# Eight written-out layers on one core: turned sums of chosen tokens, key stores on ScalarE's queue, value sums behind the queries, loops written out

## The reference

```python
probs = jax.nn.softmax(logits, axis=-2)
vals_t, idx_t = jax.lax.top_k(probs.transpose(0, 2, 1), K)
tok = jnp.take_along_axis(x, flat_idx[:, :, None], axis=1)
merged = jnp.einsum('bked,bke->bed', tok, vals)
h = jnp.einsum('bei,eih->beh', jnp.concatenate([merged, ones], -1), w1)
h = jax.nn.gelu(h, approximate=False)
o = jnp.einsum('bej,ejo->beo', jnp.concatenate([h, ones], -1), w2)
```

## Time and profile before

| | |
|---|---|
| median of 3 runs | 3224.42 us (3224.24 to 3225.77) |
| profiled execution | 3221.38 us |
| its span, first to last instruction | 3219.5 us |
| mean granted TensorE clock | 0.937 |
| busy | PE 2746.0 us (85%), DVE 1872.5 (58%), ACT 1718.8 (53%), POOL 849.9 (26%) |
| mean DMA rate | 101 GB/s over the span |

### The profile page before, as it was taken

The page is one execution under the profiler, slowest core; times in us unless marked ns, Lnnn a source line. Parts: engine busy times, 40 slices in busy tenths (PEclk is TensorE's granted clock), DMA queues, the critical chain, the costliest instruction groups (busy, mean ns, idle before and its releaser), DMA issues. The chain is left out here.

```text
span 3219.5 us, 45933 instructions
## 1 busy us (share of the span) xinstructions
PE 2746.0 (85%) x14756; PEld 1541.0 (48%) x14850; DVE 1872.5 (58%) x4755; ACT 1718.8 (53%) x2876; POOL 849.9 (26%) x957
## 2 busy tenths in 40 slices
PE   7899869969999999676799878999757888888887
PEld 4233349824444454322322246999533444444453
DVE  6777551165555654323688640111459999999953
ACT  3566421146555555111277631333149999999953
POOL 4100020020000000011200031000338888888840
PEclk8899989989999999788799998999977999999988
DMA  5111156510000000696222162999250000000011
GB/s 172 47 53 48 48 184 217 194 56 1 1 1 1 1 1 1 259 416 277 72 56 66 54 232 84 341 343 347 82 155 11 21 27 18 20 20 21 17 30 49
DMA packets 161797, 325.35 MB, mean 101 GB/s; under 512 B 29392, under 2 KB 128464, under 8 KB 138448
## 3 DMA queue, kind: packets, MB, share of 16 engines
q1 hardware_dynamic: 152112, 303.14, 27.1%
q0 software_dynamic: 4608, 12.59, 1.2%
q10 hardware_dynamic: 4896, 7.35, 0.7%
HBM read 273.71 MB, written 49.15 MB: 100 GB/s over the span
## 5 line engine op out<-in xcount | busy, mean ns | idle before, releaser
L3178 DVE TENSOR_TENSOR_SCAN L3x_behind<-L3x_first_exp,L3x_beside_scan 128x513 f32<-128x513 f32 x256 | 309.3, 1208 | 0.0
L3058 POOL TENSOR_TENSOR L3x_fade<-L3x_behind,L3x_apart 128x1024 f32<-128x1024 f32 x128 | 280.8, 2194 | 68.8 <-DVE L3x_behind L3178 44.9
L1334 ACT ACTIVATE L1x_probs<-L1x_scores,L1x_neg_max 128x512 f32<-128x512 f32 x256 | 173.5, 683 | 218.7 <-DVE L1x_neg_max L1386 218.7
L1386 DVE TENSOR_REDUCE L1x_neg_max<-L1x_scores 128x2 f32<-128x1024 f32 x128 | 156.5, 1224 | 143.9 <-PE L1x_scores L1234 143.9
L3096 ACT ACTIVATE L3x_first_exp<-L3x_scores,L3x_nm 128x512 f32<-128x512 f32 x256 | 230.6, 901 | 9.8 <-DVE L3x_nm L3170 9.7
L3124 ACT ACTIVATE L3x_probs_T<-L3x_probs_tp 128x512 f32<-128x512 f32 x256 | 206.1, 806 | 12.8 <-PE L3x_probs_tp L2986 12.8
L1667 ACT ACTIVATE L2f_hiddenT<-L2f_hidden_ps,L2f_b1s 128x128 f32<-128x128 f32 x312 | 97.3, 363 | 198.4 <-PE L2f_hidden_ps L1602 198.4
L806 DVE CUSTOM_DVE_ANT_0 L0x_masked_scores<-L0x_s,L0x_mask_q 128x512 f32<-128x512 f32 x256 | 167.1, 685 | 61.6 <-issue 55.7
L3104 ACT ACTIVATE L3x_fade<-L3x_fade,L3x_rl 128x512 f32<-128x512 f32 x256 | 199.9, 951 | 0.0
L801 DVE TENSOR_REDUCE L2x_neg_max<-L2x_s 128x1 f32<-128x512 f32 x256 | 164.7, 686 | 42.6 <-PE L2x_s L697 42.3
L3170 DVE TENSOR_REDUCE L3x_nm<-L3x_scores 128x1 f32<-128x512 f32 x256 | 172.8, 675 | 18.3 <-DMA L0f_w1s<-in_L_w 16.4
(11 more groups left out here) (545 smaller groups left out, 6222.3 us busy)
## 6 DMA issues: line engine op xcount, KB each, us to landing
L2f_w1s<-in_L_w SPq DMA_DIRECT2D x39, 1024.0 KB
L2f_w2s<-in_L_w SPq DMA_DIRECT2D x39, 1024.0 KB
L1f_w1s<-in_L_w SPq DMA_DIRECT2D x32, 1024.0 KB, 15.4
L1f_w2s<-in_L_w SPq DMA_DIRECT2D x32, 1024.0 KB, 12.7
L0f_w1s<-in_L_w SPq DMA_DIRECT2D x16, 1024.0 KB, 6.1
L0f_w2s<-in_L_w SPq DMA_DIRECT2D x16, 1024.0 KB, 5.1
L0x_q_stack<-L0x_q_parts SPq DMA_DIRECT2D x96, 64.0 KB, 2.7
L0x_k_stack<-L0x_k_parts SPq DMA_DIRECT2D x96, 64.0 KB, 2.6
```

Source lines behind the costliest of these rows:

```text
L1334: nc.scalar.activation(p[:, n % 3, h, :], s[:, n % 2, h, :], ACT.Exp, bias=nmax[:, n % 4, h:h + 1], accum_out=den[:, n % 4, h:h + 1]).then ...
L3058: nc.gpsimd.tensor_tensor(fz[:, f:f + 2, :], bs[:, fb:fb + 2, 0:S], w, ALU.mult).then_inc(y_done, 1)
L3178: nc.vector.tensor_tensor_scan(bs[:, f, :], ex[:, t, :], beside[:, 0:1].to_broadcast([P, S + 1]), 0.0, ALU.add, ALU.bypass).then_inc(f_don ...
```

## The change

The sums of the chosen tokens in L1f are made the other way around: selT is the side that is loaded into the array and x_normed streams through it, in 16 matmuls that put the experts of four batches on the partitions; DVE copies the 128x256 result (merged) and PE turns it back in two transposes. ACT and DVE no longer wait for the loads of the key jobs ahead of the first group. The key jobs get a table of places (between, first, second): no job stands between turn and down of the last group, and none behind it. Their stores move from SP to ACT, issued behind the copy of h of the group after. In norm_and_project value sums 0 move one job back and sums 2 behind all jobs, and DVE reads them likewise. With keys_made PE waits for the turned tokens of a batch only. In L3x ACT issues only the four loads of pdiff, once the weights have landed, SP issues mask, gammas and distance early, the sigmoids follow turn copies 1 to 4, two exponents copies 5 and 6 and the other two jobs 1 and 3; mask work and POOL's product stand ahead of the jobs. All the loops named above (`grouped`, `steps`, layer_norm, collect) are written out.

```diff
@@ -159,11 +159,9 @@
                 dve.wait_ge(std_done, 1)
                 nc.vector.reciprocal(rstd[:], std[:]).then_inc(chain, 1)
                 dve.wait_ge(chain, 4)
-                with dve.Fori(0, NT // 4) as r:
-                    for i in range(4):
-                        t = r * 4 + i
-                        nc.vector.tensor_scalar(c.xn[:, ds(t, 1), :], c.x[:, ds(t, 1), :], mean[:, ds(t, 1)],
-                                                rstd[:, ds(t, 1)], ALU.subtract, ALU.mult).then_inc(normed, 1)
+                for t in range(NT):
+                    nc.vector.tensor_scalar(c.xn[:, t, :], c.x[:, t, :], mean[:, t:t + 1], rstd[:, t:t + 1], ALU.subtract,
+                                            ALU.mult).then_inc(normed, 1)
                 if prepare:
                     prepare(dve)
 
...
                 loads[1](sp)
+                if beside:
+                    sp.wait_ge(*v_loaded)
+                    sp.wait_ge(*k_loaded)
+                    loads[3](sp)
                 for j, (_, m, b, _, _, _, d) in enumerate(jobs):
...
                     project(j)
                     if rope and j > NK:
                         rotate(j - 1)
-                    if masked and j in (NK + 3, NK + 5):
-                        value_sums(j - NK - 3)
+                    if masked and j == NK + 4:
+                        value_sums(0)
                 if rope:
                     rotate(NJ - 1)
+                if masked:
+                    value_sums(2)
 
             @block.scalar
             def _(act):
...
-                    if beside and 3 <= i < 7:
-                        beside.sigmoid(act, i - 3)
-                if beside:
-                    beside.exponents(act, 0)
-                if keys_made:
-                    act.wait_ge(*k_loaded)
+                    if beside and 1 <= i < 5:
+                        beside.sigmoid(act, i - 1)
+                    if beside and i in (5, 6):
+                        beside.exponents(act, i - 5)
                 if bq is not None:
                     act.wait_ge(ready, 1)
                 for j in range(NK, NJ):
                     take(j)
                     if rope and j > NK + 1:
                         leading(j - 2)
-                    if beside and j in (NK, NK + 2, NK + 4):
-                        beside.exponents(act, 1 + (j - NK) // 2)
+                    if beside and j in (NK + 1, NK + 3):
...
-                        nc.vector.tensor_scalar(am[:], count[:], 0.0, None, ALU.is_lt)
-                    if masked and j in (NK + 4, NK + 6):
-                        read_sums(j - NK - 4)
-                    if beside and j in (NK + 2, NK + 5):
-                        beside.product(dve, 1 + (j - NK) // 4)
+                    if masked and j == NK + 3 and not beside:
+                        mask_maxima()
+                    if masked and j == NK + 5:
+                        read_sums(0)
+                    if beside and j in (NK + 2, NK + 4, NK + 6):
+                        beside.product(dve, (j - NK) // 2)
                 if rope:
                     split(NJ - 2)
                     split(NJ - 1)
...
@@ -609,12 +621,7 @@
 def grouped(eng, body):
 
     U = B * H
-    for u in range(8):
-        body(u, u, u // 4)
-    with eng.Fori(1, U // 8 - 1) as r:
-        for i in range(8):
-            body(r * 8 + i, i, r * 2 + i // 4)
-    for u in range(U - 8, U):
+    for u in range(U):
         body(u, u % 8, u // 4)
 
 
...
-                                                        c.xn[:, b * TB + t, k * P:(k + 1) * P],
-                                                        selT[:, t, b * E:(b + 1) * E], start=(t == 0),
-                                                        stop=(t == TB - 1))
+                    for t in range(TB):
+                        for b in range(B):
+                            last = nc.tensor.matmul(mps[b * E:(b + 1) * E, 0:D], selT[:, t, b * E:(b + 1) * E],
+                                                    c.xn[:, b * TB + t, :], start=(t == 0), stop=(t == TB - 1))
                     last.then_inc(merged_done, 1)
+                    pe.wait_ge(merged_out, 1)
+                    for k in range(KD):
+                        last = nc.tensor.transpose(mtp[:, k, 0:P], merged[:, k * P:(k + 1) * P], c.ident[:])
+                    last.then_inc(merged_turned, 1)
 
                 @block.scalar
...
                     dve.wait_ge(mu_cleared, 1)
                     for k in range(KD):
                         nc.vector.tensor_copy(mu[:, k, :, 0:B],
-                                              mps[:, k, 0:B * E].rearrange("p (b e) -> p e b", b=B))
+                                              mtp[:, k, 0:B * E].rearrange("p (b e) -> p e b", b=B))
         with ExitStack() as ectx:
             h = c.sb(ectx, tag + "h", [P, F], F32)
...
-            def second_of(g):
-                return first_of(g) + 1 if g else 0
...
                         nc.scalar.copy(h[:, 0:HF], hps[:, 0:HF]).then_inc(h_left, 1)
                         if g:
-                            later.leading(act, second_of(g - 1))
-                        if g == G - 1:
-                            later.take(act, 2 * g - 1)
+                            for j in (second[g - 2] if g > 1 else None, between[g - 1], first[g - 1]):
+                                if j is not None:
+                                    later.store(act, j)
+                            later.leading(act, second[g - 1])
...
+                    for n in range(2 * TB):
+                        shared.collect(dve, ops, n, n % 2)
         expert_blocks(c, tag, NBLK, BLK, disp, eout, dram["L2_w1"], dram["L2_w2"], ACT.Gelu, ring, AHEAD,
                       (dram["L2_b1"], dram["L2_b2"]), block_expert)
```

More of the change, by code:

```diff
@@ L275, in _ @@
                     sp.dma_start(to, parts[:, j % R, :, :]).then_inc(stored[j % R], 16)
-                    if j == max(NK - 1, 0):
+                    if j == max(NK - 1, 0) and not beside:
                         loads[3](sp)
@@ L547, in _ @@
                 if beside:
-                    beside.product(dve, 3)
                     beside.gamma_end(dve)
+                if masked:
+                    read_sums(2)
             @block.gpsimd
@@ L595, in _ @@
                         last_part(j)
-                    if beside and j == NK + 2:
-                        beside.pool_product(pool, 0)
                 if rope:
@@ L1475, in steps @@
 def steps(eng, total, m, peel, body):
-    rounds = (total - 2 * peel) // m
-    for u in range(peel):
-        body(u, u % m)
-    with eng.Fori(0, rounds) as r:
-        for i in range(peel, peel + m):
-            body(r * m + i, i % m)
-    for u in range(peel + rounds * m, total):
+    for u in range(total):
         body(u, u % m)
@@ L2197, in _ @@
                         move(g - 1)
-                        for j in range(max(2 * g - 5, 0), 2 * g - 3):
-                            later.store(sp, j)
                     move(G - 1)
-                    for j in range(2 * G - 5, len(later.jobs)):
-                        later.store(sp, j)
-                    later.all_stored(sp)
                 @block.gpsimd
@@ L2295, in _ @@
                                              ).then_inc(g_done, 1)
-                        if g:
-                            later.take(act, first_of(g))
-                            later.leading(act, first_of(g))
-                        later.take(act, second_of(g))
+                        if first[g] is not None:
+                            later.take(act, first[g])
+                            later.leading(act, first[g])
+                        if second[g] is not None:
+                            later.take(act, second[g])
+                    later.store(act, second[G - 2])
+                    later.store(act, between[G - 1])
+                    later.all_stored(act)
                 @block.vector
@@ L2321, in _ @@
                         if g:
-                            later.split(dve, second_of(g - 1))
-                        if g == G - 1:
-                            later.split(dve, 2 * g - 1)
+                            later.split(dve, second[g - 1])
+                        if between[g] is not None:
+                            later.split(dve, between[g])
                         dve.wait_ge(o_done, g + 1)
```

98 lines of the change are left out of this document (54 added, 44 removed).

## The result

The change makes the kernel faster, by a third less than forecast: 3193.0 us (median of four, 3186.7 to 3198.8) against 3225.1 for the kernel before on the same chip, a ratio of 0.9899 (0.9882 to 0.9917). I had said 3175, 3153 to 3192: the sign was right, the size was not, and the time lies just outside the range. It is next to rival 2's number (3194), though only in part for rival 2's reasons. In two later sets of runs, on other chips, the changed kernel came out 33.0 and 29.7 us faster again.

What follows compares the result with a forecast made beforehand. L1f is bound by weights, L0x's and L3x's projections by waits then SP, attention by ACT, PE and DVE, expert blocks by PE. Terms sum to 48.5: 3221.4 - 48.5 = 3172.9, plus 3.0 is 3175.9, said 3175, range 3153 to 3192.

Steps and rivals of the forecast that it cites:

- rival 2: Gains partly hidden in L3x (12), L1f's key-job loads (2) and tail (+6): 3194; chance 0.22 for 3185 and more.
- L1f's tail and the new stores: End of L1f: project and last split go, 5.8 us, less 1.8 delay for store(11) landing: -4, ends -5.8 and +6.
- L3x: L3x's projection: last turn copy at 2364 (2362 to 2368), last store 2386.7 instead of 2403.76: -16.5, ends -12 and -19.
- layer_norm: Five layer_norm parts: written-out loops save 0.4 to 2.1 us each, 1.3 taken: -6.5, ends -2 and -10.
- L1f's sums: Sums of chosen tokens in L1f: first group 9.4 us earlier, b2 still awaited: -6.5, ends -2 and -9.4.
- Value sums of L0x: L0x's projection: PE no longer waits between jobs, last store 80.2 instead of 85.56: -5.3, ends -4 and -5.5.
- Attention loops: Attention of L2x and L0x: less idle time at group turns, -7.0 and -2.2; ends -7 to -11 together.
- Expert blocks: L2f's expert blocks: PE is busy throughout, so the loop's registers are hidden: 0.
- collect: L2f's collect: lateness comes from POOL and SP beside it, not from the loop: 0.
- L2x's earlier start: L2x: PE starts earlier by a part of one job, its queue on SP covers the rest: -0.5.

Runs made afterwards that it cites:

- e1_again: Changed kernel with the stores of key jobs 8, 11 and 14 moved one group earlier, right behind the gelu, five rounds: 3190.3 us, ratio 0.9885.

## Why the prediction was partly wrong

The forecast was 48.5 us between the profiles and 22.5 were measured. Of the 26 that are missing, L1f's tail has 8, L3x 6.4, the attention loops 3.6, layer_norm 3.1 and the start of L0x 2.3.

**L1f's tail and the new stores (the step "I take a delay of 1.8. -4")** failed. It is the largest part of the error. The sum priced one wait, that of take(15) ahead of the last gelu, with 1.8 us for which there was no row. The change puts a second one, take(12), ahead of the gelu of group 6, where the stream is full; in the sum it stood at nothing, without a reason, and only rival 2 named it. That one is what failed: ACT waited 9.31 us for store 8, and the stream got a hole of 6.6 us. The 1.8 for group 7 was a guess and came out near by luck: ACT waited 7.37 us there, but down is only 1.7 us later than its last w2 allows. Measured: +6.8 and -2.8 in the profile, +4.2 and -2.3 in the kernel with the jobs alone, for -4. With stores 8, 11 and 14 sent earlier (e1_again) the two stages take 162.2 and 17.8 us for 162.6 and 20.1 before, -2.7, and the hole is gone. So the stores behind which the gelu stood are shown as the cause of the hole; what it cost in the medians is less sure, 0 and 4.3 us.

The Trainium skill (DMA: Bandwidth & Descriptors, the paragraph on arbitration) says that each DMA engine takes turns between its queues by packets. From that I had expected a store from a queue of its own to land in a few us beside the full one. The runs don't bear my conclusion out. The eight L2x stores, which ACT's queue sends in pairs, landed 12.4 to 20.7 us after their issue (median 16.8), and the first six for L3x after a median of 11.5; the two that were waited for took 12.1 and 9.9. From SP's queue it had been 14.1. The row was the better guide.

**L3x (the step "I put the last copy at 2364")** was mis-sized. By the same distance from the stage's first value the copy came 4.8 us later than that, and past the bound (2368) by 0.8. I took pdiff's landing as 11.2 us from the row of before, though the change moves its issue behind the weights' landing and puts mask and distance beside it on another queue; it took 16.0. That mask and distance are what lengthens it is not shown by itself: with pdiff issued at once, and so ahead of both, it takes 12.1. The chain behind the copy was right: third store 11.1 us after it (9.8 in the forecast), then five jobs at 2.6. Measured -10.1 for -16.5. Issuing pdiff at once gives back 5.2 in the stage up to the first job.

**layer_norm (-6.5)** was mis-sized: -3.4 in the profile, -3.6 alone. I took 1.3 for each between a floor and DVE's gap. The parts won 0.9, 0.6, 0.3, 0.5 and 1.1. In L1f's the last copy ends 0.9 us earlier after DVE's start, but PE's next work begins 0.9 us behind that copy and not 0.3 as before; what holds it stays open.

**L1f's sums (-6.5)**: right, and right in its reason. 9.3 us are won at the sums and 3.7 go to the wait for b2, -5.6 in the profile, -6.0 alone.

**Value sums of L0x (-5.3)**: the jobs are 4.7 shorter, as worked out. Before them, the stretch from the first value to the first job is 2.3 us longer, which seven of nine traces of the changed kernel and its edits show (28.1 to 28.3) and two don't (25.7). The new order alone (25.8) and the loops alone (25.7) don't have it; where it comes from stays open.

**Attention loops (-9.2)**: the forecast of the loop is exact, and what arrives is less. From the sixteenth turn of probabilities of L2x's attention (L883, L890) to the last, all four traces with the loop have 208.1 to 208.2 us and all ten without it 201.1 to 201.2: -7.0. In L0x the same stretch is 251.4 to 251.5 and 249.2, -2.3 for -2.2. In L2x the first sixteen make up the rest, 38.3 us for 35.7 in this profile: that is the clock, below. In L0x 1.8 us are lost behind the last turn (17.2 us for 15.4; nine of the ten show it, the third trace of the changed kernel doesn't), for which I have no cause.

**Expert blocks (0), collect (0)**: right; the blocks take 289.8 us in either form. **L2x's earlier start (-0.5)** doesn't show: L2x's projection takes 61.3 us for 61.2.

**The range** reached to 3192, and the text says that it takes in rival 2, whose own number is 3194; 3185 and more had a chance of 0.22. Three of the forecast's terms (the tail, L3x, layer_norm) were guesses, and in each I took a value nearer to its good end than to its bad one. That the time came out 1 us from rival 2's number is in part luck: its landing of pdiff and its stores behind ACT's copies came true (-10.1 for its -12, and +4.0 for its +6), but its third part, the key jobs' loads in L1f, did not (-5.6 for its -2), and layer_norm and the attention fell short where it had nothing.

## What to carry over

When a change puts a wait for a transfer ahead of an instruction that feeds the bound (here a gelu that frees the buffers of a full stream), look for every place where it does so, and price each with the landing time of that transfer under that load, not with the idle one. Then set it against what the next instruction waits for anyway: of two waits of 9.3 and 7.4 us here, the first made a hole of 6.6 us in the stream and the second cost 1.7. When a load's issue moves, its landing time of before is no row for it any more. And after a stage-by-stage sum, add the terms that have no row of their own once at their bad ends: if rival and range then overlap, the range must hold that sum.

## What the runs showed of the hardware

The same kernel is 35 us faster on some chips: before runs at 3225.1 and 3224.3 us on two, at 3190.0 and 3187.9 on two others. The traces put it in L2f: from the first collect matmul to the blocks 68 us for 44, and in the late part 62 to 65 for 52 to 56, in every kernel, with a loop or without. On the two slower chips PE stands idle there for 11.3 us until DVE's read and for 7.2 with nothing named, while POOL issues 32 indirect DMAs in 40 us. On the two faster ones POOL issues the same 32 in the same 40 us, and PE has neither wait. Why only on these chips stays open.

Single executions of one program differ with the granted clock: in the three sets the fastest of the changed kernel have a mean clock of 0.938, 0.943 and 0.941 (3186.7, 3150.8 and 3185.0 us), the slowest 0.935, 0.934 and 0.933 (3198.8, 3164.8 and 3196.5). Between kernels one such stretch can be followed. The first 30 us of L2x's attention (PE busy, granted clock, DMA share, GB/s), in the kernel before:

```profile
1590.10:1620.10 30.00, 27.99 (x101) 0.65 0.10 27
```

in the changed one:

```profile
1581.20:1611.20 30.00, 28.39 (x87) 0.52 0.10 27
```

and in the one with earlier stores and later sigmoids:

```profile
1575.30:1605.30 30.00, 27.32 (x116) 0.80 0.10 27
```

PE had been idle for 15 us before each. At 0.52 nearly the whole stretch is at the 1.2 GHz level, and the attention takes 253.8 us; at 0.80 it takes 248.6, with the same instructions behind. Two kernels have the same clock there, the one with only the turned sums, which keeps the loop, and the one with only the loops written out:

```profile
1581.33:1611.33 30.00, 28.30 (x96) 0.58 0.09 27
1588.92:1618.92 30.00, 28.29 (x96) 0.58 0.09 27
```

Their attention takes 259.2 and 252.0 us: 7.2 apart, what the loop is worth. What sets the clock of this stretch is not shown; it is 0.51 or 0.52 in seven of the nine traces of the changed kernel and its edits, and 0.60 and 0.80 in the two with later sigmoids, an edit that lies only in L3x, behind this stage. So a gain of 7 us in the loop can arrive as 4.5 or 9.8, and four executions of this kernel don't settle less than some 5 us.
